# Reordered start-up and tail of a recurrent layer with a bitlinear block, and an on-chip spill fetched in 512-byte runs

## The chip, the core and the metric

The kernel runs on one core of one Trainium2 chip. The metric is the device time of one execution in microseconds, the median of several runs. The engines are TensorE (PE, matmuls), VectorE (DVE), ScalarE (ACT), GpSimd (POOL) and SyncE (SP, which issues most DMAs). Each works through its own queue in program order; semaphores join them.

## The reference

16384 tokens (64 sequences of 256) go through an embedding lookup, a minGRU-like recurrence on layer-normalised rows and a bitlinear block with a low-rank addition.

```python
h = table[ids]                                   # 16384 x 256
x = layernorm(h)
f, i, g = x @ Wf.T, x @ Wi.T, x @ Wh.T
# log-space scan in the reference; equal to
# s_t = sigmoid(f) * s_(t-1) + sigmoid(i) * max(g + 0.5, sigmoid(g)), s_0 = 0.5
h = h + s
y = layernorm(h)
r = relu(bitlinear(y, w_fc) + gate * (y @ v.T @ fast_b.T @ u.T))
out = h + bitlinear(r * r, w_proj)               # weights rounded to -1, 0, 1 times a scale per row
```

## The kernel before

The tokens are cut into N = 32 chunks of 512 columns. A step n works on chunk n's gates (f, i, g) and on chunk n-1's bitlinear block, and projects chunk n-2. Steps 0 to 4 and 29 to 32 are written out; steps 5 to 28 are a loop. The order of each engine's work in a step is written out by hand in its own `step` function, so an engine that waits holds up all that stands behind it.

- PE in a steady step: six `gate`s of eight matmuls (three, then `project(n - 2)`, then three), `low_parts` and `low_sums` for the low-rank product, `wide` (w_fc) and `narrow` (u) matmuls into four PSUM banks, and `turn_upper`. f32 values are split into two f16 parts (hi, lo), and both go through PE.
- ACT: `evict` takes a gate out of its bank (`forget`, `inp`, `cand_sig`, `cand_lin`), `normalise` and `x_high` make the layer-normalised rows and their high part, `clip` applies relu, `square_high` and `square` square pairs of 128 hidden rows.
- DVE: `guard`, `guard_sum` (limits on the gathered rows, giving h0), `measure` (statistics), `x_low`, `square_low` (the low part of the squares), `candidate`, `weigh`, `scan`, `scale_output`, `emit`, `residual`.
- POOL: `root` turns mean and variance into `shift` and `rstd` in four instructions, and gathers the embedding rows.
- SP: per step two x_cols<-x_rows transposes of the second norm, `spill_blocks`, four fetches in `fetch_rows`, two transposes of the first norm for the next step, and `store`.

The lower half of the recurrence's result goes back to row layout through DRAM: `turn_blocks` on DVE transposes 32x32 blocks into `hid_blocks`, SP writes them to `spill` and reads them with four DMAs as `hid_rows`, which `residual` adds. The upper half is transposed on PE (`turn_upper`).

Ahead of step 0 the weights are prepared: `scale_low_rank`, `turn_low_rank` (PE) and `split_low_rank` for v and fast_b, sums of |w_fc| and |w_proj| on ACT, `split_u` and `set_relu_scale`. In steps 0 and 1 the transposes of the normalised rows are made by PE (`turn_normed`, then `cols_high` on ACT and `cols_low` on DVE), later by DMA. A semaphore `gate_taken` counts evictions: gate(4) and gate(5) wait until 4 and 3 of the step have been done, in the order of `evict_low` (cand_sig, cand_lin, inp, forget).

## Time and profile before

| | |
|---|---|
| median of 3 runs | 914.6 us (913.95 to 914.6) |
| profiled execution | 913.92 us, of which the span from first to last instruction is 912.1 us |
| PE, DVE, ACT, POOL busy | 880.3, 755.8, 788.5, 418.5 us |
| mean granted TensorE clock | 0.998 |
| one clip (relu, 128x512), one square (128x1024) on ACT | 689 ns, 1066 ns |
| ACT starts to take `inp` of step 0 | 26.97 us |
| three gates back to back on PE (24 matmuls) | 5.35 us |
| one project(n) on PE (64 matmuls) | 6.99 us |
| DVE idle before the first `x_low(0, 2)`, for ACT's x_rows | 0.28 us |
| packets under 512 B | 200134 of 225372 |

An engine's busy time sums its instructions; PE's matmuls overlap, so its busy share is not a share of its peak. Times in the rows below are us from the span's start unless they are marked ns.

### The profile page before, as it was taken

The page shows a single profiled execution, that of the slowest core. Times are in us where ns is not written, and L with a number is a line of the kernel's source. Part 1 is how long each engine was busy: PE and PEld are TensorE (multiplying, and loading weights), DVE is VectorE, ACT ScalarE, POOL GpSimd, SP SyncE. Part 2 cuts the span into 40 slices and gives each one's busy share as a digit, 9 for nine tenths or more (in the row PEclk, how much of TensorE's full clock was granted, in tenths as well). Part 3 has the DMA queues.
Part 4 walks back from the last instruction along what each step waited for, and adds up shares of the span by engine and source line. Part 5 has one row for each costly group of instructions (what it writes and reads, how often), then busy time and mean ns, then how long its engine had stood idle before and what let it go on. Part 6 is the DMA issues. An engine that isn't in the chain of part 4 may idle for free.

```text
span 912.1 us, 18335 instructions
## 1 busy us (share of the span) xinstructions
PE 880.3 (97%) x5505; PEld 482.1 (53%) x5505; DVE 755.8 (83%) x1338; ACT 788.5 (86%) x1195; POOL 418.5 (46%) x457
## 2 busy tenths in 40 slices
PE   4979999999999999999999999999999999999997
PEld 2435554555555455555455555545555545555554
DVE  6988888788888888888888888888888888888766
ACT  5677998888998888998888899888889988899884
POOL 7446544445544445554444554444555444433110
PEclk9999999999999999999999999999999999999999
DMA  4123434432333443333443233344333334423311
GB/s 146 24 53 68 92 73 87 99 78 69 89 82 75 98 98 61 79 85 74 91 98 78 68 88 82 75 97 98 63 81 89 73 85 97 97 51 82 78 47 47
DMA packets 225372, 72.88 MB, mean 80 GB/s; under 512 B 200134, under 2 KB 220176, under 8 KB 225344
## 3 DMA queue, kind: packets, MB, share of 16 engines
q1 hardware_dynamic: 219200, 68.33, 33.8%
q0 software_dynamic: 6144, 4.21, 2.0%
q8 instruction: 14, 0.23, 0.1%
q14 instruction: 14, 0.11, 0.0%
HBM read 27.68 MB, written 24.64 MB: 57 GB/s over the span
## 4 chain that ended last, share of the span: by engine, by line
PE 85%; DVE 4%; ACT 4%; issue 2%; DMA 2%; SPq 1%; POOL 1%; ACTq 0%; POOLq 0%; DVEq 0%
PE bank L848 33%; PE bank L870 22%; PE y_ps L784 22%; PE bank L884 3%; PE turned L824 1%; ACT sq L584 1%; PE turned L761 1%; ACT normed L509 1%; ACT relu L571 1%; SPq L338 1%; DMA x_cols<-x_rows 1%; PE turned L772 1%; PE turned L771 1%; DMA spill<-hid_blocks 1%; DVE hid L1277 0%
## 5 line engine op out<-in xcount | busy, mean ns | idle before, releaser
L870 PE MATMUL bank<-x_cols,fc_t 128*128 128x512 f16 x1024 | 244.1, 381 | 3.6 <-ACT relu L571 3.6
L420 POOL TENSOR_SCALAR var_eps<-moments 128x4 f32<-128x4 f32 x64 | 59.5, 929 | 387.9 <-DVE moments L1020 387.6
L848 PE MATMUL bank<-x_cols,w_hi 128*128 128x512 f16 x768 | 229.8, 381 | 4.9 <-ACT forget L560 2.0
L848 PE MATMUL bank<-x_cols,w_lo 128*128 128x512 f16 x768 | 229.4, 380 | 0.0
L784 PE MATMUL y_ps<-proj_t,sq_hi 128*128 128x256 bf16 x1024 | 225.6, 273 | 3.0 <-DVE sq_lo L1203 3.0
L784 PE MATMUL y_ps<-proj_t,sq_lo 128*128 128x256 bf16 x1024 | 225.6, 273 | 0.0
L571 ACT ACTIVATE relu<-bank,relu_scale 128x512 f32<-128x512 f32 x256 | 159.3, 689 | 39.6 <-PE bank L884 39.0
L410 POOL DMA_INDIRECT rows_raw<-table,idx_now x128 | 148.0, 1156 | 59.9 <-issue 30.8
L870 PEld LDWEIGHTS bank<-x_cols,fc_t 128*128 128x128 bf16 x1024 | 95.0, 98 | 130.8 <-issue 28.3
L1203 DVE TENSOR_TENSOR sq_lo<-sq,sq_hi 128x1024 f16<-128x1024 f32 x128 | 150.6, 1214 | 5.8 <-ACT sq L584 5.7
L509 ACT ACTIVATE normed<-h,shift,rstd 128x256 f32<-128x256 f32 x256 | 132.7, 601 | 5.4 <-POOL shift L428 5.4
L584 ACT ACTIVATE sq<-relu 128x1024 f32<-128x1024 f32 x128 | 136.3, 1066 | 0.0
L578 ACT ACTIVATE sq_hi<-relu 128x1024 f16<-128x1024 f32 x124 | 132.2, 1066 | 0.0
L848 PEld LDWEIGHTS bank<-x_cols,w_lo 128*128 128x128 f16 x768 | 75.4, 98 | 91.3 <-issue 1.3
L848 PEld LDWEIGHTS bank<-x_cols,w_hi 128*128 128x128 f16 x768 | 71.6, 98 | 91.3 <-issue 8.5
L784 PEld LDWEIGHTS y_ps<-proj_t,sq_hi 128*128 128x128 f16 x1024 | 100.2, 98 | 19.7 <-issue 3.7
L1025 DVE TENSOR_TENSOR x_rows<-normed,x_rows 128x1024 f16<-128x1024 f32 x60 | 73.2, 1221 | 44.5 <-ACT x_rows L516 44.5
L784 PEld LDWEIGHTS y_ps<-proj_t,sq_lo 128*128 128x128 f16 x1024 | 100.1, 98 | 14.7
L425 POOL TENSOR_TENSOR rstd<-var_eps,minus_half 128x4 f32<-128x4 f32 x64 | 93.0, 1453 | 5.3
L1016 DVE BATCH_NORM_STATS2 stats<-h 128x6 f32<-128x256 f32 x252 | 88.3, 413 | 3.2
L1277 DVE TENSOR_TENSOR_SCAN hid<-forget,value 128x256 f32<-128x256 f32 x128 | 81.5, 678 | 5.9 <-DVE value L1263 4.6
L516 ACT ACTIVATE x_rows<-normed 128x1024 f16<-128x1024 f32 x60 | 63.4, 1057 | 4.7
(143 smaller groups left out, 919.7 us busy)
## 6 DMA issues: line engine op xcount, KB each, us to landing
out<-out_sb SPq DMA_DIRECT2D x31, 512.0 KB, 3.0
spill<-hid_blocks SPq DMA_DIRECT2D x30, 256.0 KB, 2.1
hid_rows<-spill SPq DMA_DIRECT2D x120, 64.0 KB
rows_raw<-table,idx_now POOLq DMA_INDIRECT x128, 2.6
x_cols<-x_rows SPq DMA_TRANSPOSE x120, 3.6
sq<-w_fc SPq DMA_DIRECT2D x1, 1024.0 KB, 5.5
pj_raw<-w_proj SPq DMA_DIRECT2D x1, 1024.0 KB, 4.8
out<-out_sb SPq DMA_DIRECT2D x2, 256.0 KB, 2.1
```

What stands on the lines that cost most here:

```text
L410: pool.indirect_dma_start(rows_raw[:, par, j, :], None, table, bass.IndirectOffsetOnAxis(ap=idx_now[:, par, j:j + 1], axis=0), bounds_chec ...
L425: pool.tensor_tensor(rstd[k][:, :], var_eps[k][:, :], minus_half[:, :], ALU.pow)\
L509: act.activation(normed[k][:, j, :], rows[:, j, :], ACT.Identity, bias=shift[k][:, j:j + 1], scale=rstd[k][:, j:j + 1]).then_inc(normed_re ...
L571: act.activation(relu[:, p, f % 2, :], fc_bank(f, par)[:, :], ACT.Relu, scale=relu_scale[:, f:f + 1]).then_inc(relu_ready, 1)
L578: act.activation(sq_hi[:, 2 * p:2 * p + 2, :], relu[:, p, :, :], ACT.Square).then_inc(sq_hi_ready, 1)
L584: act.activation(sq[:, p, :, :], relu[:, p, :, :], ACT.Square).then_inc(sq_ready, 1)
L784: ins = pe.matmul(y_ps[:, j, :], part[:, f, j * P:(j + 1) * P], proj_t[:, f, :], start=(f == 0 and j % 2 == 0 and part is sq_hi), stop=(f ...
L848: ins = pe.matmul(gate_bank(p, par)[:, :], w[:, k, q, :], x_part(0, par, part)[:, :, k, :], start=(k == 0 and w is w_hi and part == 0), st ...
L870: ins = pe.matmul(fc_bank(f, par)[:, :], fc_t[:, f, k, :], x_part(1, 0, part)[:, :, k, :], start=(opens and k == 0 and part == 0), stop=(n ...
L1016: dve.bn_stats(stats[k][:, j, :], rows[:, j, :]).then_inc(stats_ready[k], 1)
L1203: dve.tensor_tensor(sq_lo[:, 2 * p:2 * p + 2, :], sq[:, p, :, :], sq_hi[:, 2 * p:2 * p + 2, :], ALU.subtract).then_inc(sq_lo_ready, 1)
L1277: dve.tensor_tensor_scan(hid[:, e, at], forget[:, e, at], value[:, e, at], 0.5, ALU.mult, ALU.add).then_inc(scanned, 1)
```

## The change

1. Ahead of step 0, DVE does `scale_low_rank` before `cols_low(0)` and `split_low_rank` after `measure(0, 1)`; PE does `turn_low_rank` before gate(0) and not after it.
2. ACT's two sums of |w_proj| stand behind the first two evictions of step 0, one behind each, and no longer at the step's end.
3. For the second norm's first two chunks DVE computes `var_eps` and `minus_mean`, and POOL only the power and the product.
4. At the end of DVE's step 0 the guard and `measure` of chunk 2 stand before `split_u`; `set_relu_scale` moves behind `cols_low(1)` in step 1.
5. ACT in step 1 does `normalise(0, 2)` before `low_high(0)`, and the last pair of squares of chunk 0 moves into step 2, behind four evictions, which now run forget, inp, cand_sig, cand_lin. The waits on `gate_taken` in step 2 follow that order. DVE in step 2 does `part_low` before `scale_output`.
6. `turn_blocks` writes its blocks in another order, so that each of the four fetches reads 128 runs of 512 bytes (before 512 runs of 128 bytes), and `residual` reads `hid_rows` in permuted order.
7. project(30) and project(31) run by pairs of hidden blocks, high parts ahead of low parts; ACT makes the last high part of the last chunk from `relu` (DVE made it from `sq` before).

```diff
-                rows = spill.rearrange("(i t) (j q c) -> i t j q c", t=BLOCK, j=TILES, q=B)
+                rows = spill.rearrange("(i t) (q x) -> i q t x", t=BLOCK, q=B)
                 for i in range(B):
-                    sp.dma_start(hid_rows[:, :, BLOCK * i:BLOCK * (i + 1)],
-                                 rows[i].rearrange("t j q c -> q t j c")).then_inc(blocks_moved[par], 16)
+                    sp.dma_start(hid_rows[:, i, :], rows[i]).then_inc(blocks_moved[par], 16)
...
-                pool.wait_ge(var_ready[k], 2 * c + 2)
+                if known_below(c, 2) and isinstance(c, int) and k == 1:
+                    pool.wait_ge(var_ready_first, 2 * c + 2)
...
                     square(m, 3)
+                    if not front:
+                        act.wait_ge(y_done, m)
+                        act.activation(sq_hi[:, 6:8, :], relu[:, 3, :, :], ACT.Square).then_inc(sq_hi_last, 1)
...
+                def sum_proj(k):
+
+                    act.wait_ge(pj_in, 16)
+                    act.activation(pj_a[:, k, :], pj_raw[:, k, :], ACT.Abs, accum_out=pj_s[:, 0, k:k + 1])\
+                        .then_inc(abs_summed, 1)
...
                 if start:
                     evict(0, par, 0, 0, forget, ACT.Sigmoid)
+                    sum_proj(0)
                     evict(0, par, 0, 1, inp, ACT.Sigmoid)
+                    sum_proj(1)
                     normalise(0, 1, h0[:, 1, :, :])
...
-                    act.wait_ge(pj_in, 16)
-                    for k in range(KD):
-                        act.activation(pj_a[:, k, :], pj_raw[:, k, :], ACT.Abs, accum_out=pj_s[:, 0, k:k + 1])\
-                            .then_inc(abs_summed, 1)
...
                     evict(1, par, 1, 3, cand_lin, ACT.Identity, 0.5)
                     part_high(0)
+                    normalise(0, 2, h0[:, 0, :, :])
                     low_high(0)
-                    normalise(0, 2, h0[:, 0, :, :])
                     x_high(0, 2)
-                    back(1)
+                    for f in range(4):
+                        clip(0, f, par)
+                    for p in range(2):
+                        square_high(0, p)
+                        square(0, p)
+                        clip(0, 4 + 2 * p, par)
+                        clip(0, 5 + 2 * p, par)
+                    square_high(0, 2)
+                    square(0, 2)
                     return
                 if second:
-                    evict_low()
+                    evict(2, par, 0, 0, forget, ACT.Sigmoid)
+                    evict(2, par, 0, 1, inp, ACT.Sigmoid)
+                    evict(2, par, 0, 2, cand_sig, ACT.Sigmoid)
+                    evict(2, par, 0, 3, cand_lin, ACT.Identity, 0.5)
+                    square_high(0, 3)
+                    square(0, 3)
...
+                def tiles(part, p, rows=range(TILES)):
+
+                    for f in (2 * p, 2 * p + 1):
+                        for j in rows:
+                            ins = pe.matmul(y_ps[:, j, :], part[:, f, j * P:(j + 1) * P], proj_t[:, f, :],
+                                            start=(f == 0 and j % 2 == 0 and part is sq_hi),
+                                            stop=(f == FC - 1 and part is sq_lo), skip_group_check=True)
...
+                if isinstance(c, int) and c == N - 1:
+                    for p in range(3):
+                        high(p)
+                        low(p)
+                    high(3)
+                    for b in range(2):
+                        low(3, (2 * b, 2 * b + 1)).then_inc(y_done, 1)
                     return
...
+                if isinstance(c, int) and c == N - 2:
+                    high(0)
+                    high(1)
+                    low(0)
+                    high(2)
+                    low(1)
+                    high(3)
+                    low(2)
+                    turn_normed(1, N - 1)
+                    low(3).then_inc(y_done, 1)
+                    return
...
-                        pe.wait_ge(gate_taken, 8 * n + ((1, 2) if start else (4, 3))[p - 4])
+                        pe.wait_ge(gate_taken, 8 * n + ((1, 2) if start or second else (4, 3))[p - 4])
...
+                    dve.tensor_scalar(var_eps[k][:, :], moments[k][:, :, 1], EPS, None, ALU.add).then_inc(var_ready_first, 1)
+                    dve.tensor_scalar(minus_mean[k][:, :], moments[k][:, :, 0], -1.0, None, ALU.mult)\
+                        .then_inc(var_ready_first, 1)
...
+            scale_low_rank()
             cols_low(0)
-            scale_low_rank()
             guard(1, 64, 1)
             guard_sum(1, 1)
-            split_low_rank()
             dve.wait_ge(h0_ready, 2)
             measure(0, 1, h0[:, 1, :, :])
+            split_low_rank()
...
-                    dve.transpose(hid_blocks[:, :], hid[:, 0, :]).then_inc(blocks_ready, 1)
+                    dve.transpose(hid_blocks[:, :].rearrange("p (q j c) -> p j q c", q=B, j=TILES),
+                                  hid[:, 0, :].rearrange("p (j q c) -> p j q c", q=B, j=TILES)).then_inc(blocks_ready, 1)
...
-                        dve.tensor_tensor(h1[:, at, :, 0:P], hid_rows[:, :, :], h0[:, at, :, 0:P], ALU.add)\
-                            .then_inc(h1_low, 1)
+                        over = lambda rows: rows[:, at, :, 0:P].rearrange("p j (i c) -> p j i c", c=BLOCK)
+                        dve.tensor_tensor(over(h1), hid_rows[:, :, :].rearrange("p i (j c) -> p j i c", j=TILES),
+                                          over(h0), ALU.add).then_inc(h1_low, 1)
...
                     residual(0, 0)
-                    split_u()
-                    set_relu_scale()
                     guard(2, 64, 0)
                     guard_sum(2, 0)
+                    dve.wait_ge(h0_ready, 3)
+                    measure(0, 2, h0[:, 0, :, :])
+                    split_u()
...
                 if first:
-                    measure_next()
                     cols_low(1)
+                    set_relu_scale()
...
                 if second:
                     x_low(0, 3)
+                if second:
+                    part_low()
                 scale_output(n - 2)
-                part_low()
+                if not second:
+                    part_low()
```

ACT in steps 0 and 1, before: the rows start with the sums of |w_fc| (`sq,fc_s`).

```order
L490 ACTIVATE sq,fc_s<-sq 128x256 x8
L560 ACTIVATE forget<-bank,w_back 128x512
L560 ACTIVATE inp<-bank,w_back 128x512
L509 ACTIVATE normed<-h,shift,rstd 128x256 x4
L560 ACTIVATE cand_sig<-bank,w_back 128x512
```

The same place in the changed kernel.

```order
L494 ACTIVATE sq,fc_s<-sq 128x256 x8
L564 ACTIVATE forget<-bank,w_back 128x512
L630 ACTIVATE out_sb,pj_s<-pj_raw 128x1024
L564 ACTIVATE inp<-bank,w_back 128x512
L630 ACTIVATE out_sb,pj_s<-pj_raw 128x1024
L513 ACTIVATE normed<-h,shift,rstd 128x256 x4
L564 ACTIVATE cand_sig<-bank,w_back 128x512
```

The sums (`out_sb,pj_s`) are new here; they stood between the scaling of `fc_b` and step 1's evictions.

DVE from the end of step 0's residual to the first low part in step 1, before. `u...` is split_u, `bound` to `grow` is set_relu_scale, `rows_fin` and `h` the guard of chunk 2.

```order
L1020 BN_AGGR moments<-stats 128x2 x4
L1121 SCALAR_TENSOR_TENSOR u<-u,u_inv 128x128
L1124 CAST u_hi<-u 128x128
L1127 COPY u_parts<-u_hi 128x32x16
L1128 TENSOR_TENSOR u_parts<-u,u_hi 128x32x16
L1134 TENSOR_REDUCE bound<-y_ps 128x1
...
L1144 TENSOR_TENSOR grow<-grow 128x1
L1004 TENSOR_SCALAR rows_fin<-rows_raw 128x1024
L1010 SCALAR_TENSOR_TENSOR h<-rows_raw,rows_fin 128x1024
L1035 TENSOR_TENSOR x_cols<-turned,x_cols 128x512 x2
```

The same stretch of the changed kernel.

```order
L1066 BN_AGGR moments<-stats 128x2 x4
L1070 TENSOR_SCALAR var_eps<-moments 128x4
L1071 TENSOR_SCALAR minus_mean<-moments 128x4
L1050 TENSOR_SCALAR rows_fin<-rows_raw 128x1024
L1056 SCALAR_TENSOR_TENSOR h<-rows_raw,rows_fin 128x1024
...
L1173 SCALAR_TENSOR_TENSOR u<-u,u_inv 128x128
...
L1180 TENSOR_TENSOR u_parts<-u,u_hi 128x32x16
L1087 TENSOR_TENSOR x_cols<-turned,x_cols 128x512 x2
L1186 TENSOR_REDUCE bound<-y_ps 128x1
```

Two small instructions came in behind the aggregates, and the set_relu_scale group moved behind `x_cols`.

ACT from step 1's last squares through step 2's evictions, before.

```order
L578 ACTIVATE sq_hi<-relu 128x1024
L584 ACTIVATE sq<-relu 128x1024
L560 ACTIVATE cand_sig<-bank,w_back 128x512
L560 ACTIVATE cand_lin<-bank,w_back 128x512
L560 ACTIVATE inp<-bank,w_back 128x512
L560 ACTIVATE forget<-bank,w_back 128x512 x2
```

The same place in the changed kernel.

```order
L564 ACTIVATE forget<-bank,w_back 128x512
L564 ACTIVATE inp<-bank,w_back 128x512
L564 ACTIVATE cand_sig<-bank,w_back 128x512
L564 ACTIVATE cand_lin<-bank,w_back 128x512
L582 ACTIVATE sq_hi<-relu 128x1024
L588 ACTIVATE sq<-relu 128x1024
L564 ACTIVATE forget<-bank,w_back 128x512
```

Four evictions moved ahead of the last pair of squares, and `forget` stands first among them.

## Rows read from the trace of the kernel before

**Rows 1.** The page, chain that ended last, shares of the span by engine.

```profile
PE 85%; DVE 4%; ACT 4%; issue 2%; DMA 2%; SPq 1%; POOL 1%; ACTq 0%; POOLq 0%; DVEq 0%
```

**Rows 2.** Busy time by stretch: stretch, its us, busy us (instructions), clock, DMA.

```profile
97.75:878.40 780.65, 779.74 (x4930) 429.60 (x4930) 655.45 (x1124) 700.43 (x1040) 363.47 (x384) 1.00 0.38 82
```

**Rows 3.** What PE waited for: us in total, times, longest us.

```profile
PE turned L730 <- ACT normed L509: 4.3, 2, 3.6
PE bank L870 <- ACT relu L571: 3.6, 3, 2.0
PE y_ps L784 <- DVE sq_lo L1203: 3.0, 5, 1.2
PE turned L761 <- DVE x_cols L1035: 2.3, 1, 2.3
PE bank L848 <- ACT forget L560: 2.0, 2, 1.3
...
PE bank L848 <- DMA x_cols<-x_rows: 1.5, 2, 0.8
```

**Rows 4.** Timeline of DVE and ACT, 23 to 41 us: start, us, instruction, idle before.

```profile
23.23 1.23 DVE L1010 SCALAR_TENSOR_TENSOR h<-rows_raw,rows_fin 128x1024 f32<-128x1024 f32 x1
25.11 0.19 DVE L1056 CAST a_hi<-y_ps 128x32 f16<-128x32 f32 x1 [0.66 <-PE y_ps L712]
...
25.52 1.39 DVE L1016 BATCH_NORM_STATS2 stats<-h 128x6 f32<-128x256 f32 x4
...
29.72 2.08 ACT L509 ACTIVATE normed<-h,shift,rstd 128x256 f32<-128x256 f32 x4 [2.06 <-POOL shift L428]
...
39.98 1.04 ACT L634 ACTIVATE out_sb<-pj_raw 128x1024 f32<-128x1024 f32 x1
```

**Rows 5.** Timeline of DVE, 46.8 to 53 us.

```profile
46.80 0.28 DVE L1134 TENSOR_REDUCE bound<-y_ps 128x1 f32<-128x128 f32 x1
...
47.97 0.70 DVE L1004 TENSOR_SCALAR rows_fin<-rows_raw 128x1024 f32<-128x1024 f32 x1
...
51.70 1.25 DVE L1035 TENSOR_TENSOR x_cols<-turned,x_cols 128x512 f16<-128x512 f32 x2
```

**Rows 6.** Timeline of ACT, 57 to 63 us.

```profile
57.06 0.60 ACT L548 ACTIVATE low_hi<-turned 128x512 f16<-128x512 f32 x1 [2.78 <-PE turned L772]
...
60.61 2.41 ACT L571 ACTIVATE relu<-bank,relu_scale 128x512 f32<-128x512 f32 x4
```

**Rows 7.** Timelines of DVE and PE, 63 to 89 us.

```profile
63.32 1.27 DVE L1277 TENSOR_TENSOR_SCAN hid<-forget,value 128x256 f32<-128x256 f32 x2
...
80.97 1.23 DVE L1025 TENSOR_TENSOR x_rows<-normed,x_rows 128x1024 f16<-128x1024 f32 x1 [1.09 <-ACT x_rows L516]
...
88.59 0.38 PE L771 MATMUL turned<-part_hi,spread 128*128 128x512 f16 x1 [0.56 <-DVE part_lo L1307]
```

**Rows 8.** SP's timeline, the chain in order of time, and PE's timeline.

```profile
85.60 0.34 SPq L330 DMA_DIRECT2D spill<-hid_blocks  x1
87.97 4.59 SPq L338 DMA_DIRECT2D hid_rows<-spill  x4
...
94.52 3.19 DMA x_cols<-x_rows
...
152.47 0.60 PE L848 MATMUL bank<-x_cols,w_hi 128*128 128x512 f16 x2 [0.83 <-DMA x_cols<-x_rows]
```

**Rows 9.** ACT's timeline and the chain near the end.

```profile
900.42 2.05 ACT L584 ACTIVATE sq<-relu 128x1024 f32<-128x1024 f32 x2
...
903.65 2.91 PE y_ps L784 x24
```

**Rows 10.** Busy time by stretch, 53.00 to 55.80 us; clock after POOL's busy time.

```profile
53.00:55.80 2.80, 2.79 (x10) 0.98 (x11) 1.46 (x3) 0.60 (x1) 1.85 (x5) 0.50 0.00 0
```

**Rows 11.** Timeline of DVE in a steady step.

```profile
138.06 0.71 DVE L1284 STREAM_TRANSPOSE hid_blocks<-hid 128x512 f32<-128x512 f32 x1
...
141.41 0.69 DVE L1307 TENSOR_TENSOR part_lo<-turned,part_hi 128x512 f16<-128x512 f32 x1 [1.53 <-ACT part_hi L542]
```

More of the change, by code:

```diff
@@ L779, in project @@
                     pe.wait_ge(u_ready, 2)
-                def tile(f, j):
-                    for part in (sq_hi, sq_lo):
-                        ins = pe.matmul(y_ps[:, j, :], part[:, f, j * P:(j + 1) * P], proj_t[:, f, :],
-                                        start=(f == 0 and j % 2 == 0 and part is sq_hi),
-                                        stop=(f == FC - 1 and part is sq_lo), skip_group_check=True)
-                    return ins
-                halves = isinstance(c, int) and c == N - 1
@@ L790, in project @@
-                for f in range(FC):
-                    if isinstance(c, int) and c == N - 2 and f == FC - 2:
-                        turn_normed(1, N - 1)
-                    if f % 2 == 0:
-                        pe.wait_ge(sq_hi_ready, 4 * c + f // 2 + 1)
-                        pe.wait_ge(sq_lo_ready, 4 * c + f // 2 + 1)
-                    if halves and f == FC - 2:
-                        break
-                    for j in range(TILES):
-                        ins = tile(f, j)
-                if not halves:
-                    ins.then_inc(y_done, 1)
-                    return
@@ new lines, in high, with low @@
+                def high(p):
+                    if isinstance(c, int) and c == N - 1 and p == 3:
+                        pe.wait_ge(sq_hi_last, 1)
+                    else:
+                        pe.wait_ge(sq_hi_ready, 4 * c + p + 1)
+                    return tiles(sq_hi, p)
+                def low(p, rows=range(TILES)):
+                    pe.wait_ge(sq_lo_ready, 4 * c + p + 1)
+                    return tiles(sq_lo, p, rows)
+                if isinstance(c, int) and c == N - 1:
[5 more added lines that the diff above has]
+                        low(3, (2 * b, 2 * b + 1)).then_inc(y_done, 1)
+                    return
@@ new lines, in project @@
+                if isinstance(c, int) and c == N - 2:
[9 more added lines that the diff above has]
+                    return
+                for p in range(4):
+                    pe.wait_ge(sq_hi_ready, 4 * c + p + 1)
+                    pe.wait_ge(sq_lo_ready, 4 * c + p + 1)
+                    for f in (2 * p, 2 * p + 1):
+                        for j in range(TILES):
+                            for part in (sq_hi, sq_lo):
+                                ins = pe.matmul(y_ps[:, j, :], part[:, f, j * P:(j + 1) * P], proj_t[:, f, :],
+                                                start=(f == 0 and j % 2 == 0 and part is sq_hi),
+                                                stop=(f == FC - 1 and part is sq_lo), skip_group_check=True)
@@ L897, in step @@
                         pe.wait_ge(x_landed[0], 32 * (n - 1))
-                    gate(0)
-                    if start:
-                        turn_low_rank()
-                    gate(1)
-                    gate(2)
+                    for p in range(3):
+                        gate(p)
                     if first:
@@ L1198, in square_low @@
                 dve.wait_ge(sq_ready, 4 * m + p + 1)
[L1199 removed]
+                last = isinstance(m, int) and m == N - 1
+                if last and p < 3:
                     dve.wait_ge(y_done, m)
                     dve.tensor_copy(sq_hi[:, 2 * p:2 * p + 2, :], sq[:, p, :, :]).then_inc(sq_hi_ready, 1)
[L1202 removed]
+                if last and p == 3:
+                    dve.wait_ge(sq_hi_last, 1)
+                else:
+                    dve.wait_ge(sq_hi_ready, 4 * m + p + 1)
                 dve.tensor_tensor(sq_lo[:, 2 * p:2 * p + 2, :], sq[:, p, :, :],
@@ L1251, in candidate @@
                 def candidate(e):
-                    dve.wait_ge(gate_taken, 8 * n + (8 if e else 4 if start else 2))
+                    dve.wait_ge(gate_taken, 8 * n + (8 if e else 4 if start or second else 2))
                     dve.tensor_tensor(cand[:, e, :], cand_lin[:, e, :], cand_sig[:, e, :], ALU.max)\
@@ L1260, in weigh @@
                     if e == 0:
-                        dve.wait_ge(gate_taken, 8 * n + (2 if start else 3))
+                        dve.wait_ge(gate_taken, 8 * n + (2 if start or second else 3))
                     wait(dve, scanned, 4 * (n - 1) + 2 * e + 2)
@@ L1269, in scan @@
                     if e == 0:
-                        dve.wait_ge(gate_taken, 8 * n + (1 if start else 4))
+                        dve.wait_ge(gate_taken, 8 * n + (1 if start or second else 4))
                     if e == 0 and steady:
```

32 lines of the change are left out of this document (17 added, 15 removed).

## Prediction

> **What bounds the kernel now.** I read the chain that ended last first: TensorE (PE) holds 85% of it [rows 1]. Then the busy time by stretch: from 97.75 us (step 3) to 878.40 us PE is busy 779.74 of 780.65 us [rows 2]. Nothing that another engine does in those 29 steps can shorten them, except for the 0.91 us that is left. So what can be gained lies before 97.75 us and after 878.40 us. The list of what PE waited for names it [rows 3]: 4.3 us for `normed`, 3.6 us for `relu` banks, 3.0 us for `sq_lo`, 2.3 us for `x_cols` from VectorE (DVE), 2.0 us for `forget` banks (0.7 in step 1, 1.3 in step 2), 1.5 us for `x_cols` by DMA. One of the two DMA waits, 0.83 us, is at 152.47 us inside the steady stretch [rows 8]; the other, some 0.6 us, stands before step 3's first gate at 97.75 us.
>
> I followed PE's order through the start, asking at each station what ends last there, and how much earlier that comes after the change. The gains don't add by themselves: each station takes the smallest of what its releasers give.
>
> **Station A, second chunk's transposes: 1.03 us.** Before, DVE finished h0 of chunk 1 (23.23 + 1.23 = 24.46 us), then idled 0.66 us for PE's small low-rank products, split them, and began `stats` at 25.52 us; ScalarE (ACT) could normalise only at 29.72 us, straight after POOL [rows 4]. Now the low-rank split stands behind `stats`, which starts at some 24.49 us: 25.52 - 24.49 = 1.03 us earlier at `normed`, and at everything up to step 1. The five small DVE instructions that scale the low-rank product move ahead of cols_low(0), and the PE products ahead of gate(0). I cost them at nothing: DVE and PE are both waiting there for ACT's `x_cols` copies; without that cover they cost about 1 us on DVE. The sums of w_proj go behind the first two evictions: each is 1.04 us of ACT, the second stands behind the eviction of `inp`, which was taken at 26.97 us (table) and comes no later now: 26.97 + 0.57 + 1.04 = 28.6 us at the latest. normed can start at 29.72 - 1.03 = 28.7 us, so ACT waits for POOL anyway. If that cover were gone, the cost is 1.04 us at most.
>
> **Station B, first chunk's low-rank part: 1.95 us.** The sums no longer stand before step 1's evictions, so the 0.7 us wait for `forget` in step 1 goes [rows 3]. PE gives it back at once: it waits next for `normed` of h1, then for `x_cols` from DVE. Between step 0's residual and `x_cols` at 51.70 us DVE had no break; set_relu_scale, from 46.80 to 47.97 us, is the part that moves behind `x_cols` [rows 5]: minus 1.17 us. The two tiny instructions (var_eps, minus_mean) that POOL loses and DVE gains cost about 0.25 us. So 1.03 + 1.17 - 0.25 = 1.95 us, and PE's low_parts, which starts when `x_cols` ends (51.70 + 1.25 = 52.95 us), starts at 51.0 us. POOL's root gets shorter by some 0.5 us, which is hidden: DVE, not ACT, is last.
>
> **Station C, wide(4) and turn_hidden(1): 2.25 us.** low_high now stands behind normalise(0,2). Before, ACT did low_high at 57.06 us, then 3.1 us of normalise and x_high, and the first `relu` came at 60.61 us [rows 6], for which PE idled 2.0 us [rows 3]. Now normalise fits into ACT's 2.78 us wait for the low sums [rows 6], low_high comes at 57.06 - 1.95 = 55.1 us, and x_high ends about 56.7 us. PE's narrow, which the first `relu` needs, ended at about 60.61 + 0.7 - 2.0 = 59.3 us and comes 1.95 us earlier; its first bank is done a little sooner, so `relu` starts about 57.2 us: 3.4 us earlier. But DVE becomes the next thing late. Its chain from low_lo to the scan that ends at 63.32 + 1.27 = 64.59 us [rows 7] moves by 1.95 us plus an idle 0.28 us (table) that vanishes, so turn_hidden(1) starts at 62.4 us. PE, which met the scan's end without a wait before (64.6 us), is there at 61.2 us now and waits 1.2 us: a new wait. Gain 2.25 us.
>
> **Station D, step 2's gates: 3.55 us.** The evictions now stand before the last square pair, in the order forget, inp, candidate. gate(4) needs only `forget`: ACT has 8 `relu` and 6 squares before it from 57.2 us, at 0.69 and 1.07 us (table) no more than 11.9 us, so it is taken by 69.8 us. gate(3) ends later: 2.25 us earlier than before, near 71.7 us (gate(4) started some 1.3 us after it, and a gate takes 1.73 us by the table). The 1.3 us wait [rows 3] is gone: 2.25 + 1.30 = 3.55 us at project(0). The late square pair is hidden: the last `sq_lo` hangs on DVE's own chain, ended at 80.97 - 1.09 = 79.88 us before [rows 7] and 2.0 us earlier now, and PE wants that pair three quarters through project(0), which takes 7.0 us from about 75.1 us: at 80.4 us.
>
> **Station E, low_parts of step 2: 3.1 us.** Here DVE and SP decide again. x_low(1,1) ran from 80.97 us after 1.09 us idle [rows 7]; DVE's part comes 2.25 - 0.25 us earlier, ACT's `x_rows` 3.4 us. The idle time goes too: 2.0 + 1.1 = 3.1 us, a new PE wait of about 0.45 us. Then part_low no longer stands behind scale_output, so the 0.56 us wait at low_sums [rows 7] goes; against it ACT's x_high(0,3), tied to POOL, comes only about 3.5 us earlier in this round. I take 3.5 us for what follows.
>
> **Station F, step 3: 4.1 us.** SP issues spill, four fetches, then the transposes. The fetches take 4.59 us from 87.97 us, and the second transpose lands at 94.52 + 3.19 = 97.71 us [rows 8]. With 128 runs of 512 bytes each instead of 512 runs of 128, what does an issue cost? No row shows it. From below: the spill, 128 runs, takes 0.34 us, so four take 1.4 us; from above: they stay at 4.59 us. The spill is nearest in runs, so I take 4 x 0.5 = 2 us. The transposes then land about 97.71 - 3.1 - 2.5 = 92 us, before PE wants them at 97.13 - 3.5 = 93.6 us. The other wait goes as well: 97.75 - 93.6 = 4.1 us. By the upper bound they land at 94.6 us, and 1.0 us is lost.
>
> **Inside the steady stretch: 0.83 us.** The same fetches delay the transposes before 152.47 us [rows 8]; freed of over 2 us they land in time. Otherwise steps stay PE's: the spill's transpose on DVE (0.71 us) and the residual get other access patterns, of unchanged size. No row shows that pattern, so the bounds are unchanged and some times slower (a rival below); a gain there is excluded, since PE doesn't wait.
>
> **The end: 0.55 us.** For project(30) PE's two waits for `sq_lo` (1.2 and 1.0 us of rows 3) are filled with high parts, but low_parts then waits for `x_cols`, which hangs on ACT's unbroken row of squares and normalise: 0.1 us. For project(31), DVE loses one 0.7 us cast to ACT, which has ended by then. Before, 24 matmuls followed sq_lo of pair 2 (903.65 us, 2.91 us) until the first half was done [rows 9]; now ACT squares once more after 900.42 + 2.05 = 902.4 us, so sq_lo of pair 3 is ready near 902.4 + 1.0 + 1.2 = 904.6 us, in time, and low(2), high(3) and half of low(3), 20 matmuls, follow: 4 x 0.11 = 0.44 us.
>
> **Sum.** 4.1 + 0.83 + 0.55 = 5.5 us off the profiled execution: 913.92 - 5.5 = 908.4 us. The median before is 0.7 us above that execution; half of it added gives 908.9 us.
>
> **A rule against it.** PE's granted clock was 0.50 from 53.00 to 55.80 us [rows 10], the 1.2 GHz level, after idling 2.3 us and eight transposes that went at ACT's pace. These 2.8 us at half pace cost 1.4 us against 2.4 GHz. The same gaps stand there after the change, so I change nothing. If the restart ran at 2.4 GHz, up to 1.4 us more would be gained; if the low level lasted through the next eight matmuls, about 1.3 us would be lost; both are bounds of the range. The Trainium skill (TensorE: Matmul & The Clock Gate, "Loop structure matters more than you think") says that a loop with long waits between matmuls lets PE go cold. By it the new waits at stations B and C could bring more of the slow level: 910.2 instead of 908.9 us.
>
> **Rivals.**
> 1. The fetches cost SP what they did, because the issue time follows the bytes and not the runs. For: the four differ little in work from before, 64 KB each. Against: the spill moves 256 KB in 0.34 us. Stations F and the steady wait give back 1.0 + 0.83: 910.7 us. Chance 0.12.
> 2. The clock restarts later, or a tie (station C or E) breaks by a microsecond the wrong way: 910.2 us. Chance 0.15.
> 3. The clock doesn't fall, or DVE's new wait is shorter: 907.5 us. Chance 0.10.
> 4. The start's gain is taken back before step 3 by a wait I don't see, and only the tail and some fetch time stay: 913 us, no measurable change. Against: every queue has slack in steady steps, and PE keeps what it is given [rows 2]. Chance 0.03.
> 5. Slower: DVE's transpose writing four scattered groups of 32 columns per block row, at 0.71 us now, becomes slow. It is followed by 1.53 us of DVE idle before part_low [rows 11], and PE wants part_lo about 0.35 us later; up to 1.9 us more cost nothing. From there each microsecond counts in 29 steps. At 0.71 + 1.9 + 0.2 = 2.8 us it has eaten the gain; at 3.2 us the time is 926 us. The size in and out is the same and no row hints at a fourfold cost. Chance 0.03.
> The forecast itself has 0.57.
>
> **How the numbers follow.** A measurement of this kernel tells a change of about 0.2%, 1.8 us, from none. Faster by more than that: the forecast and rivals 1 to 3, 0.94; within it: rival 4, 0.03; slower 0.03. The range goes from the lucky clock (908.9 - 1.9) to rivals 1 and 2 with a part of both, 911.3 us.
>
> **What would show it.** Right: DVE `stats` of chunk 1 near 24.5 us; low_parts near 51.0 us; a PE wait of about 1.2 us for the scan near 62.4 us; no `forget` wait in step 2; hid_rows issues near 0.5 us each; step 3's first gate near 93.6 us without a wait; a stretch to the start of the last steps equally long less 0.8 us. Wrong: fetch issues near 1.15 us, a stretch of clock 0.50 longer than 3 us, the DVE transpose or residual above 0.75 us, or PE waits from step 4 on.

## The result, and the profile after

The changed kernel took **924.51 us** (median of 5 runs, 923.27 to 924.66) against 914.6 us before (5 runs, 913.92 to 914.9): ratio 1.0107, 95% interval 1.0096 to 1.0118. It is slower by 9.9 us, where 5.7 us less had been forecast. The profiled execution took 923.27 us, with a span of 921.5 us against 912.1.

Chain of the changed kernel, then what PE waited for (us in total, times, longest), as in [rows 1] and [rows 3]:

```profile
PE 65%; ACT 17%; DVE 6%; issue 6%; another core or an unknown queue 2%; POOL 1%; DMA 1%; ACTq 1%; SPq 0%; DVEq 0%; POOLq 0%
```

```profile
PE turned L796 <- DVE part_lo L1365: 14.3, 11, 1.3
...
PE turned L754 <- ACT normed L513: 4.5, 3, 3.0
PE turned L786 <- DVE x_cols L1087: 2.4, 2, 1.8
...
PE bank L897 <- DVE x_cols L1087: 1.4, 2, 0.7
PE y_ps L810 <- ACT sq_hi L582: 0.9, 1, 0.9
```

The forget wait and both `x_cols` DMA waits are gone, as forecast. New is the first row, 14.3 us. One of its 11 waits, 1.16 us, stands in step 2; the other ten stand in the loop. Busy time from step 3's first gate to the same matmul of the last steps says what that costs (stretch, its us, PE's busy us first):

```profile
94.95:886.92 791.97, 778.81 (x4924) 428.93 (x4922) 654.71 (x1117) 699.09 (x1037) 360.61 (x384) 1.00 0.38 80
```

The same stretch before was 97.75 to 876.67 us, 778.92 us long. So the change won 97.75 - 94.95 = 2.80 us ahead of it, lost 13.05 us in it, and won 35.43 - 34.54 = 0.89 us behind it (from the ends of these stretches to the ends of the spans, 912.10 and 921.46 us). The ten waits stand in steps 8, 10, ... 24 and 28 (odd steps, and steps 6 and 26, have none; in step 6 part_hi is 0.25 us late, which PE does not feel). Step 8, by PE, ACT and POOL:

```profile
245.05 0.40 PE L786 MATMUL turned<-x_cols,low_a 128*32 128x512 f16 x4
...
248.60 0.38 PE L796 MATMUL turned<-part_hi,spread 128*128 128x512 f16 x1 [1.32 <-DVE part_lo L1365]
```

```profile
244.29 0.67 ACT L564 ACTIVATE forget<-bank,w_back 128x512 f32<-128x512 f32 x1
247.13 0.60 ACT L546 ACTIVATE part_hi<-turned 128x512 f16<-128x512 f32 x1 [2.17 <-remote]
```

```profile
241.15 1.15 POOL L411 DMA_INDIRECT rows_raw<-table,idx_now  x1 [0.89 <-POOL idx_now L402]
242.60 1.01 POOL L411 DMA_INDIRECT rows_raw<-table,idx_now  x1 [0.30 <-issue]
243.91 0.99 POOL L411 DMA_INDIRECT rows_raw<-table,idx_now  x1 [0.30 <-issue]
245.21 1.00 POOL L411 DMA_INDIRECT rows_raw<-table,idx_now  x1 [0.30 <-issue]
```

PE's low_parts runs from 245.05 us and should be done at 245.45, by its modelled end. ACT has been free since 244.96 us and starts part_hi, which waits for low_parts, at 247.13 us, 1.7 us late. DVE's part_lo and PE's low_sums follow, and the step takes 1.5 us more than its neighbours: the next low_parts stands at 273.38 us, 28.3 us on, where steps 6 to 7 and 7 to 8 took 26.9. "remote" means that the profile knows no releaser. The trace also holds the update of the semaphore that low_parts increments and part_hi waits for: it is recorded 2.06 us after low_parts starts, 0.02 us ahead of part_hi, against 0.43 us in a run without the delay (run 15 below). So it is the increment that comes late, not ACT that sees it late. I call this a late completion. In odd steps part_hi starts 0.45 us after low_parts does. Nothing of PE's, ACT's or SP's own work is late here, so the prediction's suspects (the transpose, the residual, the fetches) explain nothing: the residual takes 0.69 us and the transpose 0.71 us, as before. One of its signs of being wrong, "PE waits from step 4 on", did come true.

### The profile page after: what moved, and what is told of

The parts are those of the page before. It is cut to its first block, busy times and chain, and to the rows that moved or that the text cites. A ratio compares the mean times of both kernels' runs of the same rounds, so it can differ in the third digit from the quotient of the medians.

```text
span 921.5 us, 18330 instructions
## 1 busy us (share of the span) xinstructions
PE 880.9 (96%) x5505; PEld 482.7 (52%) x5505; DVE 757.4 (82%) x1341; ACT 788.9 (86%) x1196; POOL 413.1 (45%) x453
## 4 chain that ended last, share of the span: by engine, by line
PE 65%; ACT 17%; DVE 6%; issue 6%; another core or an unknown queue 2%; POOL 1%; DMA 1%; ACTq 1%; SPq 0%; DVEq 0%; POOLq 0%
PE bank L897 22%; PE bank L919 22%; PE y_ps L853 14%; ACT normed L513 5%; ACT sq L588 4%; PE bank L933 4%; ACT relu L575 2%; ACT sq_hi L582 2%; PE turned L873 1%; ACT forget L564 1%; PE turned L796 1%; DVE part_lo L1365 1%; ACT cand_lin L564 1%; PE turned L786 1%
## 5 line engine op out<-in xcount | busy, mean ns | idle before, releaser
L853 PE MATMUL y_ps<-proj_t,sq_lo 128*128 128x256 bf16 x960 | 211.2, 273 | 0.0
L853 PE MATMUL y_ps<-proj_t,sq_hi 128*128 128x256 bf16 x960 | 211.2, 273 | 0.0
L411 POOL DMA_INDIRECT rows_raw<-table,idx_now x128 | 142.8, 1116 | 59.8 <-issue 31.6
L853 PEld LDWEIGHTS y_ps<-proj_t,sq_hi 128*128 128x128 f16 x960 | 94.0, 98 | 14.1
L853 PEld LDWEIGHTS y_ps<-proj_t,sq_lo 128*128 128x128 f16 x960 | 93.9, 98 | 14.0
```

Source lines behind the costliest of these rows:

```text
L411: pool.indirect_dma_start(rows_raw[:, par, j, :], None, table, bass.IndirectOffsetOnAxis(ap=idx_now[:, par, j:j + 1], axis=0), bounds_chec ...
L853: ins = pe.matmul(y_ps[:, j, :], part[:, f, j * P:(j + 1) * P], proj_t[:, f, :], start=(f == 0 and j % 2 == 0 and part is sq_hi), stop=(f ...
```

## The experiments

The runs fall into six groups. Each ran on one chip at one time, beside runs of the kernel before, whose median there was 913.3 to 914.25 us. Each is told with its own ratio to those. In the first four groups the changed kernel did not run untouched. Counts of PE's waits for part_lo include one in step 2 (0.5 to 1.3 us), which every kernel here has.

**First group: which part of the change?**

Run 1, only the 512-byte fetches, with the transpose and residual that go with them, in the kernel before:
```
-  sp.dma_start(hid_rows[:, :, 32*i:32*(i+1)], rows[i].rearrange("t j q c -> q t j c"))
+  sp.dma_start(hid_rows[:, i, :], rows[i])
```


> The kernel before with the new block layout alone: hid_rows of [P, B, TILES*BLOCK], the fetch in 512-byte runs, the transpose and the residual in that order. In the trace of the changed kernel, PE waits 1.32 us in 10 even steps of the loop (low_sums for part_lo), because ACT's part_hi starts 1.7 us late. Theory 1 (the layout: shorter fetches and other transfers beside low_parts delay what releases part_hi) expects those waits here: some 10 of 1.3 us, and 914.6 + 13 - 2 = about 925 us. Theory 2 (the numbers of the semaphores, moved by two new ones) and theory 3 (where the loop stands in time or in the program after the new start) expect no such wait and 914.6 minus 1 to 2 us, about 913 us.

Measured: 911.65 us, ratio 0.9969 (0.9958 to 0.9981), and no late completion. The four fetches are issued in 2.35 us in place of 4.59 [rows 8], and the steady stretch is full:

```profile
88.72 2.35 SPq L338 DMA_DIRECT2D hid_rows<-spill  x4
```

```profile
97.73:874.84 777.11, 777.11 (x4924) 429.71 (x4922) 654.16 (x1117) 699.01 (x1037) 362.45 (x384) 1.00 0.38 82
```

That is 1.8 us shorter than before. Theory 1 (the layout) falls.

Run 2, the changed kernel with the old layout. 

> The changed kernel with the block layout of before alone (128-byte runs, fetch issues of over 4 us). Theory 1 expects that the ten waits of 1.3 us are gone: 924.5 - 13 + 2 = about 913 us. Theories 2 and 3 expect them still there: about 925 to 926 us.

Measured: 920.11 us (913.55 to 923.58), ratio 1.0063 (1.0040 to 1.0086), nine waits for part_lo. Most of the waits stay without the new layout, so the loss is not in it.

Run 3, the changed kernel with its two new semaphores declared last, run 4 the kernel before with them declared, unused, in the changed kernel's places:
```
+  var_ready_first = sem("var_ready_first")    # run 3: behind stored; run 4: behind var_ready
+  sq_hi_last = sem("sq_hi_last")              # run 3: behind stored; run 4: behind sq_hi_ready
```


> The changed kernel with its two new semaphores declared last, so that every other semaphore has the number that it had before. Not one instruction moves. Theory 2 (numbers) expects that the ten waits are gone: about 911 us. Theories 1 and 3 expect 924.5 us as before.

> The kernel before with the same two semaphores declared, unused, where the changed kernel has them. Theory 2 expects the ten waits to appear: 914.6 + 13 = about 928 us. Theories 1 and 3 expect 914.6 us, unchanged.

Measured: run 3 917.4 us, ratio 1.0031 (1.0019 to 1.0043), six waits for part_lo, 5.3 us; run 4 913.9 us, ratio 0.9999. The waits are there in run 3 and not in run 4: theory 2 (numbers) falls. Runs 2 and 3 have fewer or shorter waits than the changed kernel, and I have no cause for how many. The trace of run 3 shows that the gathers' place does not decide it. Steps 10 and 16, POOL's last gather and ACT's part_hi; low_parts starts at 299.61 and 462.19 us, 0.18 us ahead of the gather in both:

```profile
299.79 1.00 POOL L411 DMA_INDIRECT rows_raw<-table,idx_now  x1 [0.30 <-issue]
301.61 0.60 ACT L546 ACTIVATE part_hi<-turned 128x512 f16<-128x512 f32 x1 [2.08 <-remote]
...
462.37 1.00 POOL L411 DMA_INDIRECT rows_raw<-table,idx_now  x1 [0.30 <-issue]
462.82 0.60 ACT L546 ACTIVATE part_hi<-turned 128x512 f16<-128x512 f32 x1 [0.71 <-PE turned L786]
```

part_hi comes 2.00 us behind low_parts in one and 0.63 in the other.

**Second group: the place in DVE's program.** Laying the traces of these runs side by side gave theory 4, which the next expectation states. Its rows are DVE's value and POOL's first gather in step 8, before and after (the changed kernel's gather is shown above):

```profile
243.86 0.69 DVE L1254 TENSOR_TENSOR cand<-cand_lin,cand_sig 128x512 f32<-128x512 f32 x1
244.74 0.69 DVE L1263 TENSOR_TENSOR value<-inp,cand 128x512 f32<-128x512 f32 x1 [0.19 <-DVE cand L1254]
```

```profile
244.87 1.60 POOL L410 DMA_INDIRECT rows_raw<-table,idx_now  x1 [0.89 <-POOL idx_now L401]
```

```profile
240.14 0.69 DVE L1310 TENSOR_TENSOR cand<-cand_lin,cand_sig 128x512 f32<-128x512 f32 x1
241.14 0.73 DVE L1319 TENSOR_TENSOR value<-inp,cand 128x512 f32<-128x512 f32 x1 [0.30 <-DVE cand L1310]
```

Before, value starts 0.13 us ahead of the gather, which then takes 1.60 us. After, value starts 0.11 us later against its cand, at the same 0.01 us as the gather, and the gather takes 1.15 us; the three that follow come 0.45 us earlier. The Trainium skill (SBUF — State Buffer, "SBUF: two separate sides") says that DVE and GpSimd share one pair of ports as an exclusive lock, which the one that starts first keeps for its whole instruction; among the DVE instructions that take it are those with two SBUF inputs, against a GpSimd instruction that reads SBUF. The trace agrees in part: a gather that starts 0.13 us behind value, which has two inputs, takes 0.45 us longer than one that starts with it. But when they start together neither is held up much (value takes 0.73 us and not 0.69, the gather 1.15), and what the page's rule makes of such a tie no run here shows.

Run 5, three more instructions in DVE's program in the start-up, run 6 eleven (two waits fit in one instruction):
```
   dve.reciprocal(w_inv[:, :], w_back[:, :]).then_inc(w_inv_ready, 1)
+  for _ in range(5):          # run 6: 21
+      dve.wait_ge(w_in[0], 16)
```


> The changed kernel with three more harmless wait instructions in VectorE's program, behind the reciprocal in the start-up, where DVE idles. Nothing else moves. In every run of the changed kernel so far DVE's value instruction of the loop's second step starts 0.11 us (the first time 0.35 us) later after the wait ahead of it than in the kernels built from before; POOL's first gather then starts first and takes 1.15 us in place of 1.60, the other gathers come 0.45 us earlier, and in those steps PE's completion of low_parts is seen 0.2 to 1.7 us late by ACT. Theory 4 (place in the program: the late start comes from where the instruction lies in DVE's program, which is 5 instructions longer ahead of the loop) expects the late start to move to another instruction: no waits, 924.5 - 13 = about 911 us. Theory 5 (the state in which the new start hands over to the loop, not the place) expects no change: 922 to 925 us.

> The same with 11 more wait instructions, so that DVE's loop lies 16 instructions (1 KB) behind its place in the kernel before. Theory 4 expects value to start in time, gathers of 1.60 us and about 911 us, theory 5 922 to 925 us.

Run 7, the kernel before with five. 

> The kernel before with five more wait instructions in DVE's program at the same place, so that its loop lies where the changed kernel's lies. Theory 4 expects the late value, gathers of 1.15 us in the even steps and PE waits of up to 1.3 us there: slower than before, up to 914 + 13 = 927 us. Theory 5 expects 914 us, unchanged.

Run 8, the gathers held back until value is done:
```
   fetch_index(n + 3, 1 - par)
+  pool.wait_ge(value_ready, 2 * n + 1)
+  pass_on(pool, pool_passed, n)
   gather(n + 3, 1 - par)
```


> The changed kernel with one more wait on POOL in each steady step: the four gathers start only when DVE's value of the step's first half is done, 0.5 us or more later than now. DVE's program is untouched, so its late start stays. If it is the early gathers that hold up PE's completion (theory 4's second link), the ten waits are gone: about 911 us. If the late start of value itself or something else is the cause, they stay: 924 us.

Measured: run 5 908.79 us, ratio 0.9944 (0.9927 to 0.9961); run 6 909.73, 0.9954; run 8 908.59, 0.9941 (0.9924 to 0.9958); run 7 913.37, 0.9999. In run 5 the step-8 gather takes 1.59 us again and value's idle time is 0.19 us, so an instruction's place does decide when it starts. Run 7 brings the late value into the kernel before (0.31 us of idle time, gathers of 1.16 us), but not one late completion, and its expectation of a loss fell. I took this for a second condition in the program. The fifth group shows that it was not, and with it that the three times of 908.6 to 909.7 us say nothing of the ten waits: the changed kernel takes 909.0 us on such a chip without any of these edits.

**Third and fourth group: a second condition in the program?**

Run 9, the changed kernel with four more instructions ahead of POOL's loop (run 14: twelve, in run 7's kernel):
```
   pool.wait_ge(consts_ready, 3)
+  for _ in range(9):          # run 14: 25
+      pool.wait_ge(raw_cleared, 1)
```


> The changed kernel with four more wait instructions in POOL's program in the start-up, so that POOL's loop lies where it lay before (the change takes four instructions from POOL); DVE's place stays that of the changed kernel, so value starts late and the gathers come early. With DVE alone moved (five more waits in the kernel before) the gathers came early too, and yet no completion was late. Theory 6 (POOL's place in its program is the second thing that is needed) expects no waits: about 910 us. Theory 7 (the second thing lies in the start-up's timing or in the new order of root's waits) expects 920 to 925 us as before.

Run 10, the kernel before with the change's root and measure (var_eps and minus_mean of two chunks on DVE), which alone puts both loops where the change puts them. 

> The kernel before with one part of the change: var_eps and minus_mean of the first two h1 chunks on DVE, and root's waits in the new order. DVE's loop then lies 5 instructions and POOL's loop minus 4 instructions from their places before, exactly where they lie in the changed kernel. Theory 6 expects early gathers, late completions and PE waits of up to 1.3 us in even steps: 918 to 927 us. Theory 7 with the start-up's timing expects about 914 us; with root's new order it expects 918 to 927 us too.

Run 11, run 8's kernel, with this ahead of step 2's gather:
```
+  if isinstance(n, int) and n == 2:
+      pool.wait_ge(part_hi_ready, n)
```


> The changed kernel with the gathers held back as before (908.6 us), and in step 2 held back until part_hi is under way. There, too, ACT sees low_parts 0.97 us late while a gather starts 0.34 us behind it, and PE waits 1.2 us for part_lo. If an early gather is the cause there as well, that wait falls to 0.3 us or less and the time to about 907.8 us; if the cause is another, it stays and the time is 908.6 us.

Measured: run 9 913.09 us (910.35 to 918.28), ratio 0.9993 (0.9974 to 1.0012), late completions in every even loop step but 6 and 26, and six waits for part_lo; run 10 919.28 us, ratio 1.0046 (1.0028 to 1.0064), with eight waits for part_lo; run 11 908.62 us, ratio 0.9942 (0.9926 to 0.9959), no late completion and no wait in the loop. The three, in this order:

```profile
PE turned L798 <- DVE part_lo L1367: 4.7, 6, 1.2
PE turned L775 <- DVE part_lo L1319: 8.0, 8, 1.2
PE turned L801 <- DVE part_lo L1370: 1.2, 1, 1.2
```

Run 9 has the late completions with POOL's loop in its old place, so theory 6 falls, though its time lies between the two expectations. Run 10 has them without the rest of the change, so theory 7 is left with the order of root's waits. Run 11's value still starts late (0.31 us of idle time), so the gathers are what counts. Its step 2 kept the wait of 1.2 us for part_lo: there PE's completion is in time, and ACT is busy, so that expectation missed.

Run 12, run 7's kernel with the new order of root's two waits (run 13 the reverse, in the changed kernel):
```
-  pool.wait_ge(moments_ready[k], TILES * (c + 1))
   wait(pool, normed_ready[k], TILES * c)
+  pool.wait_ge(moments_ready[k], TILES * (c + 1))
```


> The kernel before with DVE's program moved by five instructions (early gathers, 913.4 us, no late completion) and, on top, the changed kernel's order of POOL's two waits in root: normed_ready first, then moments_ready. Theory 7 (the order of the waits is the second condition) expects late completions in even steps and 917 to 925 us. If POOL's place or the moved instructions are the second condition, 913.4 us.

Run 13, the changed kernel with the old order. 

> The changed kernel with the old order of those two waits in the loop; no place in any program moves. Theory 7 expects no PE wait for part_lo in the loop and about 910 us; otherwise 920 to 925 us as before.

Run 14, POOL's program moved by twelve. 

> The kernel before with DVE's program moved by five instructions and POOL's by twelve, which is minus four to the next multiple of sixteen, where the changed kernel's POOL program stands. Theory 6 (POOL's place is the second condition, and it counts in sixteens) expects late completions and 917 to 925 us; otherwise 913.4 us.

Measured: 913.46 us (1.0000), **909.05 us** (0.9949, 0.9933 to 0.9966) and 913.61 us (0.9996). Run 13 looked like the answer, the order of two waits, though run 12 beside it has that order, early gathers and no late completion, which theory 7 did not allow. It was not the answer. All runs with early gathers had late completions in groups one and three, and none in groups two and four, whatever the kernel. The traces of groups one and three also held fewer records of semaphore updates by DMA (3,767 to 4,429 against some 5,800). What I had read as a condition of the program was one of the chip, or of its state at the time; "the chip reacts" stands for either here. The profiles that this case began with stand on both sides, too: 5,813 records in the kernel before, 3,752 in the changed one. The kernel before, whose gathers come late, takes nearly the same on both (913.9 to 914.3 us in groups one, three and six, 913.3 to 913.7 in the others).

**Fifth and sixth group: the same two kernels once more.** Runs 15 and 18 are the changed kernel as it is, runs 16 and 17 are run 7's kernel. The record gives chip number 9 for both groups; it does not tell whether that was one chip in two states or two chips of that number in two machines.

> The changed kernel as it is, once more, on another chip. Theory 8 (the second condition is the chip: the late completions come only on some chips, those whose traces record few DMA semaphore updates) expects either some 3800 such records and 918 to 925 us with the waits, or some 5800 and about 909 us without one wait for part_lo in the loop, although the gathers come early. Theory 7 (order of the waits) expects 920 to 925 us wherever it runs.

> The kernel before with DVE's program moved by five waits, once more. Theory 8 expects: where run 15 is slow, this is slower than before too, by 3 to 10 us; where run 15 is fast, 913.5 us. Theory 7 expects 913.5 us in either case.

> The kernel before with DVE's program moved by five waits, on a third chip. If the chip is of the kind of chips 7 and 15 (some 3800 DMA semaphore records in the trace), theory 8 expects late completions in even steps and 917 to 924 us; if it is of the kind of 6, 9 and 12 (some 5800), 913 us.

> The changed kernel as it is, on the same chip as run 17. Theory 8 expects 918 to 925 us with some 3800 records, or 909 us with some 5800.

| | fifth group | sixth group |
|---|---|---|
| kernel before | 913.3 us | 913.86 us |
| changed kernel, untouched | **908.96** (0.9957, 0.9941 to 0.9974) | **924.06** (1.0117, 1.0099 to 1.0135) |
| before, DVE moved by five | 912.69 (0.9998) | **925.3** (1.0127, 1.0109 to 1.0145) |
| DMA semaphore records | 5,824 and 5,805 | 3,748 and 3,811 |

Theory 8 holds in both groups (run 17 came out 1.3 us above its range), and theory 7 falls. Step 8 of the changed kernel in run 15, ACT and then POOL, against the same step above:

```profile
244.91 0.67 ACT L564 ACTIVATE forget<-bank,w_back 128x512 f32<-128x512 f32 x1
246.12 0.60 ACT L546 ACTIVATE part_hi<-turned 128x512 f16<-128x512 f32 x1 [0.54 <-PE turned L786]
```

```profile
241.77 1.15 POOL L411 DMA_INDIRECT rows_raw<-table,idx_now  x1 [0.89 <-POOL idx_now L402]
243.23 1.00 POOL L411 DMA_INDIRECT rows_raw<-table,idx_now  x1 [0.30 <-issue]
244.54 1.00 POOL L411 DMA_INDIRECT rows_raw<-table,idx_now  x1 [0.30 <-issue]
245.84 0.99 POOL L411 DMA_INDIRECT rows_raw<-table,idx_now  x1 [0.31 <-issue]
```

low_parts starts at 245.67 us there, so the last gather stands 0.17 us behind it, against 0.16 in the profile of the result. The gathers lie alike, to 0.01 us, and part_hi starts 0.45 us behind low_parts in place of 2.08. In run 17 the kernel before, with nothing of the change in it but a program of DVE five instructions longer, shows the changed kernel's loss:

```profile
PE turned L771 <- DVE part_lo L1309: 13.4, 11, 1.4
```

## Why the prediction was wrong

**The step that failed** is in "Inside the steady stretch: 0.83 us": "Otherwise steps stay PE's", with rival 4's "PE keeps what it is given". The stretch was to get 0.83 us shorter and got 13.05 us longer (14.87 us longer than in run 15), by ten PE waits of 1.3 us for part_lo. I had looked there only for an engine with more work. What moved was the place of DVE's loop in its program.

Shown, each within one group: five more instructions on DVE, and so early gathers, cost 11.4 us where the chip reacts to them (run 17). Holding the gathers back in the changed kernel leaves no late completion there (run 11, 908.62 us); the nearest kernel beside it that has early gathers is run 9, 4.5 us slower. Where the chip does not react, the untouched changed kernel takes 908.96 us, a gain of 4.3 us on the kernel before beside it, where 5.7 us had been forecast; run 5, which has late gathers anyway, takes 908.8. The chip that gave the result reacts.

Not shown: by what way gathers near low_parts hold up PE's completion, and what sets the two kinds of places apart. The chip's number does not: number 9 stood on both sides. The traces with late completions are also those that lack semaphore records, so that the recording itself has a part in the delay is a rival that no run here tests. The changed kernel with DVE's loop moved by three was run only where the chip does not react. That the time could get longer at all had a chance of 0.03 in the prediction, by another mechanism (rival 5).

**Points of the forecast**, by the profiled run after, and run 15 for the loop:

| station | forecast | measured |
|---|---|---|
| A: turn_normed(0,1), 30.37 to 29.54 us | 1.03 | 0.83 |
| B: low_parts, 53.01 to 52.10 | 1.95 | 0.91 |
| C: turn_hidden(1), 64.65 to 63.34 | 2.25 | 1.31 |
| D: project(0), 78.72 to 75.94 | 3.55 | 2.78 |
| E: low_sums, 88.59 to 86.59 | 3.5 | 2.00 |
| F: step 3's first gate, 97.75 to 94.95 | 4.1 | 2.80 |
| steady stretch, 778.92 to 777.10 | 0.83 | 1.82 (run 15) |
| end | 0.55 | 0.89 |

The forecast sum was 5.5, and 2.80 + 1.82 + 0.89 is 5.5 too. That agreement is luck twice over: the misses cancel, and the terms come from two executions. Run 15 taken alone reaches step 3 only at 95.67 us, so that its span gained 2.08 + 1.82 + 0.87 = 4.8 us. That the time of 908.96 us stands next to the forecast's 908.9 (the sum gives 908.8) is luck as well: the kernel before took 913.3 us there and not 914.6. At A, POOL's power took 1.36 us and not 1.18, the missing 0.2 us. The first large miss: I carried A's 1.03 us on into B. DVE's rows of the changed kernel show that it never arrived.

```profile
24.54 1.41 DVE L1062 BATCH_NORM_STATS2 stats<-h 128x6 f32<-128x256 f32 x4
...
31.22 1.68 DVE L1162 TENSOR_SCALAR bound_b<-ones,bound 128x128 f32<-128x128 f32 x1
32.87 0.20 DVE L1164 RECIPROCAL u_inv<-u_max 128x8 f32<-128x8 f32 x1
32.99 0.64 DVE L1310 TENSOR_TENSOR cand<-cand_lin,cand_sig 128x512 f32<-128x512 f32 x1
...
42.42 1.22 DVE L1357 TENSOR_TENSOR h<-turned,h 128x1024 f32<-128x1024 f32 x1
...
45.53 0.17 DVE L1070 TENSOR_SCALAR var_eps<-moments 128x4 f32<-128x4 f32 x1
...
50.76 1.28 DVE L1087 TENSOR_TENSOR x_cols<-turned,x_cols 128x512 f16<-128x512 f32 x2
```

stats comes 0.98 us earlier (25.52 in [rows 4]). But bound_b takes 1.68 us where it took 0.27, beside POOL's gather and memset, and cand starts where it did before, at 32.97. ACT had finished its `cand_lin` at 32.11 us, so cand could have started 0.8 us earlier. From there DVE has no break as far as x_cols, so only what left that stretch counts: 51.70 [rows 5] less 50.76 is 0.94 us, the 1.17 of set_relu_scale less 0.23 for var_eps and minus_mean, as priced. Some 0.8 to 1.0 us is missing from then on. At E, low_parts does not wait, but part_hi comes late from ACT's own queue: ACT starts the normalise ahead of it only at 81.42 us, after 1.96 us of waiting for POOL. So low_sums waits 1.16 us where I had forecast no wait, and the miss grows to 1.5 us.

The second miss is to the good: the steady stretch holds 1.82 us and not 0.83. PE's busy time in it fell as well, from 778.01 to 777.10 us; run 1 shows that the fetches alone give all of it. The end gave its 0.89 us ahead of project(31), which starts with high parts and no longer waits 0.48 us for sq_lo, and nothing behind it.

**Right were** that the forget wait and both DMA waits go, the new wait for the scan (0.80 us at 63.34, forecast 1.2 at 62.4), the issue of four fetches (2.24 to 2.35 us, forecast 2; rival 1 falls), the transpose and residual at their old length (rival 5's mechanism falls), and the clock:

```profile
52.10:54.90 2.80, 2.80 (x10) 0.98 (x11) 2.44 (x10) 2.13 (x5) 1.93 (x3) 0.50 0.97 186
```

The granted clock falls to 0.50 for 2.8 us from low_parts on, as in [rows 10], and is 0.99 or more again from 54.90 us to step 3. The new waits of 0.8 us did not bring the slow level back, nor did the 1.16 us at E, so the clock's half of rivals 2 and 3 did not happen. Of their other halves something did: station E's tie broke the wrong way by 1.2 us (rival 2), and the new wait for the scan was 0.4 us shorter than forecast (rival 3).

## What to carry to other kernels

An edit ahead of a loop also moves the loop: in the program of each engine, where 0.1 us on one DVE instruction was enough to let the other engine go first. When a loop gets slower in which no instruction changed, look for the first instruction that starts late against its own neighbours, then pad the program by a few instructions before blaming the edit. A wait that fixes the order of two engines (run 8's two lines) can take such a tie out of the time: the changed kernel with it takes 908.6 us in both groups where it ran (runs 8 and 11), one of them on a chip that shows the loss, and is as fast as the best of the others (908.8 to 909.1 us).

Compare only kernels that ran on one chip at one time, and run the unchanged kernels again there: I built theories on places and on an order of two waits out of runs from four chips, and one repeat of the changed kernel brought them down.

## What the runs showed of the hardware

- PE's semaphore increment can come 0.2 to 1.7 us after the matmuls end, while gathers are issued on POOL. It was seen only in some groups, with the last gather starting between 0.2 us ahead of low_parts (run 10, step 6) and 0.33 us behind it (the changed kernel, step 6). That phase is not enough: in run 17's step 6 and in run 4's step 3 the last gather starts 0.06 and 0.05 us behind low_parts, and part_hi is in time.
- With the last gather in one place to 0.01 us, the delay still differs from step to step in one execution: in run 3's trace part_hi starts 0.62 to 2.03 us behind low_parts over ten loop steps with the gather at 0.17 or 0.18 us.
- DVE's value, at one place of its program, starts 0.11 us late in each pass of the loop, 0.35 us in the first; three or eleven instructions more ahead of the loop take the delay away (runs 5 and 6), five more bring it into the kernel before (run 7).
